# Query rows turned a stage early, the first queries sent back at once, ScalarE normalising, the row of maxima ahead of the last store

## The chip, the cores and the metric

One core of a Trainium2 chip runs the whole kernel. The metric is the device time of one execution in microseconds. The kernel before takes 3972.45 us, the median of three runs (3970.11 to 3986.83).

## The reference

A decoder layer on x of shape (4, 1024, 512): a self-attention against given keys and values, a cross-attention of 16 heads over a context of 1601 rows per batch, and a feed-forward part with 8 experts, each added to x. Only the front of the cross-attention matters here:

```python
x = x + self_attention(layernorm(x), k, v)
q = split_heads(layernorm(x) @ Wq.T + Wq_b)        # 4096 x 512
k = split_heads(ctx @ Wk.T + Wk_b)                 # 4 x 1601 x 512
v = split_heads(ctx @ Wv.T + Wv_b)
scores = where(mask == 0, -1e9, q @ k.T / sqrt(32))
x = x + (softmax(scores) @ v) @ Wo.T + Wo_b
```

where layernorm(x) = (x - mean) / sqrt(var + 1e-5) over each row, without learned factors.

## The kernel before

The kernel is a chain of blocks. At the end of a block all engines meet at a barrier; SP reaches it only when its DMAs have landed. Three blocks matter.

**The context stage** (`context_keys_values`, tiles named cxl_). For each of 4 batches and 4 groups q of 384 (the last 449) context rows, PE turns the rows of the next group (`turn`, L810), multiplies for the keys (`keys`, four products of 12 matmuls each) and for the values (`values`). Every fp32 number is held as a high and a low float32r part, so each product is three matmuls (`matmul3`, L44 to L46). ACT takes the high part out of PSUM, DVE the low part, and `finish_v` (DVE, L909) adds the bias of the values. SP stores keys and values. Two blocks of 512 rows of x1 for the next stage are loaded here (`q_rows`, the tensors probs) and normalised by DVE in the last batch. Before ACT and DVE begin they wait for both bias vectors (`bias_in`); DVE raises `cT_low` only behind that wait, and PE's first `turn` waits for `cT_low`.

**The query projection** (`project_queries`, tiles named pql_). 8 steps s of 512 rows, each with 4 products hd of 12 matmuls (one per chunk of 128 query columns). In step s PE also turns the rows of step s + 1, one 128-row piece (`turn`, L1160) ahead of each product. ACT takes the high part of the turned piece (`high`, L1208), DVE the low one (`low`, L1235), DVE adds the bias to a product (`query`, L1243), ACT makes the high half of that (L1219), POOL the low half (`split_q`, L1139), and SP stores a whole step's queries (L1118). DVE also takes the mean and variance of the rows of step s + 2 at hd 0 (`statistics`, L956 to L961), POOL the power -0.5 of it, and DVE normalises the four pieces at hd 2 (`normalize`, L967). The rows of step 0 are turned at the start of the block, ahead of the first product.

Inside this block the first maxima of the cross-attention are found too: 64 slots, each one matmul of scores (`mx`, L1013) and one DVE reduction (`read`, L1020). They need the keys of head group 0 (`load_keys`) and the first 512 queries of batch 0, which SP reloads from DRAM out of chunk 0 (`load_queries`, L999). Three slots go with each hd from step 2 on:

```python
FIRST_MX, SLOTS_AT = 2, 3
n = SLOTS_AT * (DC * (s - FIRST_MX) + hd)
```

At the end SP stores the last step's queries, then sends the row of maxima to DRAM (L1124) and back into the queries' tile (`put_row`, L1005), and waits for all of it.

**The cross-attention** (tiles named xa_) starts behind that barrier with the scores of unit 0 (L1476). SP's queue works in the order of its program: what stands behind a wait there is not sent before it. The name queries is one tensor that holds, by turns, the context's turned rows, the query weights and the queries of a head group.

## Time and profile before

| What | Value |
|---|---|
| Median of 3 runs (lowest, highest) | 3972.45 us (3970.11, 3986.83) |
| The profiled execution, its own time | 3982.51 us |
| Its span | 3980.7 us |
| Busy: PE | 3805.0 us (96%) |
| Busy: DVE, POOL, ACT | 2418.8, 1484.6, 1425.7 us |
| Mean granted clock of PE | 0.982 of full |

Times of a row are microseconds from the span's start. In a timeline a row is the start, the length, the engine and line, the operation, output <- inputs and their shapes; in brackets stands how long the engine was idle before it, and what ended that. A row with x4 is four instructions merged. SPq is SP's queue that issues DMAs. A row of a tile gives least/median/greatest length in ns. In a table of stretches each engine has its busy time and count, then come PE's granted clock as a share of full speed, the mean busy share of the 16 DMA engines and what they moved.

### The profile page before, as it was taken

To read this page: it belongs to the slowest core of one execution; us is meant where nothing else is said; L and a number is where in the kernel's file an instruction comes from. 1 tells how busy PE (TensorE), PEld (TensorE's weight loads), DVE (VectorE), ACT (ScalarE), POOL (GpSimd) and SP (SyncE) were. 2 spreads that over 40 slices of the span, in tenths; PEclk is the share of its full clock that TensorE was granted. 3 is DMA by queue.
4 is the path that set the end of the run, shared out by engine and by line. 5 is a ranking of instruction groups with operands and counts; after the bars stand their busy time and mean duration, and the time that the engine had idled before them with its cause. 6 is when DMAs were issued, how large, how long until landed. Compare 5 with 4: busy or idle time off the path is not lost. (4 is left out here: it accounts for less than half of the span.)

```text
span 3980.7 us, 63499 instructions
## 1 busy us (share of the span) xinstructions
PE 3805.0 (96%) x19001; PEld 2545.6 (64%) x19161; DVE 2418.8 (61%) x6240; ACT 1425.7 (36%) x1769; POOL 1484.6 (37%) x836
## 2 busy tenths in 40 slices
PE   8999999999987899999999999999999999988997
PEld 6888888888875444444444444444444777766875
DVE  6444444444447587888888888888887533424235
ACT  3112212133222344555545555545554312113332
POOL 1000000000012577666677666677664122220033
PEclk9999999999999999999999999999999999998999
DMA  4000000155554422221122222222202343237588
GB/s 153 32 32 32 32 32 32 61 169 178 196 159 146 110 53 56 56 50 34 40 47 55 56 56 56 56 53 55 56 20 81 124 147 111 102 107 265 163 291 282
DMA packets 224580, 381.59 MB, mean 96 GB/s; under 512 B 17448, under 2 KB 101960, under 8 KB 224332
## 3 DMA queue, kind: packets, MB, share of 16 engines
q1 hardware_dynamic: 197100, 309.73, 26.9%
q0 software_dynamic: 13120, 43.00, 3.0%
q10 hardware_dynamic: 14112, 25.70, 1.7%
q8 instruction: 137, 2.24, 0.2%
q14 instruction: 111, 0.91, 0.1%
HBM read 229.71 MB, written 148.66 MB: 95 GB/s over the span
## 5 line engine op out<-in xcount | busy, mean ns | idle before, releaser
L1020 DVE CUSTOM_DVE_ANT_0 xf_unread<-xa_mx_ps,mask_q 128x402 bf16<-128x402 f32 x1984 | 1034.4, 574 | 297.7 <-PE xa_mx_ps L1013 168.2
L1608 ACT ACTIVATE probs<-xa_scores 128x1024 f32<-128x1024 f32 (+1 forms) x416 | 417.2, 1023 | 417.4 <-PE xa_scores L1482 377.2
L1608 ACT ACTIVATE xa_probs<-xa_scores 128x1024 f32<-128x1024 f32 (+1 forms) x416 | 417.1, 1023 | 400.9 <-PE xa_scores L1482 353.2
L1443 POOL TENSOR_TENSOR xa_sums<-xa_sums,xa_probs 128x1024 f32<-128x1024 f32 x220 | 519.5, 2381 | 18.1 <-POOL xa_sums L1443 14.6
L1443 POOL TENSOR_TENSOR xa_sums<-xa_sums,probs 128x1024 f32<-128x1024 f32 x220 | 519.1, 2380 | 19.0 <-POOL xa_sums L1443 14.5
L1482 PE MATMUL xa_scores<-mask_t,ident_b 128*128 128x512 bf16 (+1 forms) x1505 | 500.8, 388 | 5.3 <-issue 0.2
L1013 PE MATMUL xa_mx_ps<-xa_kp,queries 96*128 96x402 f32 x1024 | 366.4, 419 | 0.8
L1013 PE MATMUL xa_mx_ps<-xf_kp,queries 96*128 96x402 f32 x960 | 343.2, 419 | 3.9 <-DVE xf_maxima L1020 3.6
L1476 PE MATMUL xa_scores<-queries,xf_kp 97*128 97x512 f32 (+1 forms) x832 | 285.0, 424 | 20.7 <-ACTq L1630 13.3
L1013 PEld LDWEIGHTS xa_mx_ps<-xa_kp,queries 96*128 96x128 f32 x1024 | 181.7, 189 | 171.3 <-DVE xf_maxima L1020 111.5
L1476 PE MATMUL xa_scores<-queries,xa_kp 97*128 97x512 f32 (+1 forms) x832 | 284.7, 423 | 1.8 <-ACT probs L1608 1.8
L1482 PEld LDWEIGHTS xa_scores<-mask_t,ident_b 128*128 128x128 bf16 (+1 forms) x1664 | 123.0, 100 | 244.9 <-issue 212.3
L1013 PEld LDWEIGHTS xa_mx_ps<-xf_kp,queries 96*128 96x128 f32 x960 | 171.0, 189 | 163.4 <-DVE xf_maxima L1020 106.1
L248 POOL TENSOR_TENSOR sa_rstd<-sa_var,sa_power 128x1 f32<-128x1 f32 x32 | 17.6, 550 | 674.1 <-DVE sa_var L433 674.1
L380 ACT ACTIVATE sa_pT_high<-sa_pT_ps 128x512 fp32r<-128x512 f32 x128 | 73.0, 596 | 532.8 <-PE sa_pT_ps L298 532.8
L44 PE MATMUL sa_scores<-weights,sa_nT_high 128*128 128x512 f32 x512 | 205.5, 401 | 7.5 <-DVE sa_nT_low L441 7.5
L44 PE MATMUL sa_o_ps<-sa_v_high,sa_pT_high 128*128 128x512 f32 x512 | 208.9, 408 | 1.1 <-DVE sa_pT_low L458 1.1
L1476 PEld LDWEIGHTS xa_scores<-queries,xf_kp 97*128 97x128 f32 (+1 forms) x832 | 149.5, 187 | 87.4 <-ACT xa_probs L1608 26.0
L46 PE MATMUL sa_scores<-weights,sa_nT_low 128*128 128x512 f32 x512 | 204.1, 399 | 0.0
L45 PE MATMUL sa_scores<-queries,sa_nT_high 128*128 128x512 f32 x512 | 203.6, 398 | 0.0
L46 PE MATMUL sa_o_ps<-sa_v_high,sa_pT_low 128*128 128x512 f32 x512 | 200.6, 392 | 0.0
L45 PE MATMUL sa_o_ps<-sa_v_low,sa_pT_high 128*128 128x512 f32 x512 | 199.3, 389 | 0.0
(382 smaller groups left out, 7377.1 us busy)
## 6 DMA issues: line engine op xcount, KB each, us to landing
ex_src<-sorted_in SPq DMA_DIRECT2D x78, 256.0 KB
sorted_out<-ex_made ACTq DMA_DIRECT2D x78, 256.0 KB
queries<-qT_high SPq DMA_DIRECT2D x30, 512.0 KB
xf_kp<-kT_high SPq DMA_DIRECT2D x16, 800.5 KB
xa_kp<-kT_high SPq DMA_DIRECT2D x16, 800.5 KB
rows<-in_ctx SPq DMA_DIRECT2D x16, 768.0 KB, 4.7
values<-cxl_v SPq DMA_DIRECT2D x48, 256.0 KB
kT_high<-cxl_kT_high SPq DMA_DIRECT2D x12, 768.0 KB
```

What stands on the lines that cost most here:

```text
L44: pe.matmul(out, lh, rh, start=start, stop=False)
L45: pe.matmul(out, lh, rl, start=False, stop=False)
L46: return pe.matmul(out, ll, rh, start=False, stop=stop)
L248: pool.tensor_tensor(rstd[:, :], var[:, :], power[:, :], ALU.pow).then_inc(root, 1)
L380: act.activation(pT[0][:, j * KB:(j + 1) * KB, :], pT_ps[j % 2][:, :, :], ACT.Copy).then_inc(pT_high, 1)
L1013: return pe.matmul(out[:, 0:MKEYS], qp[0:MAXROW, j, first:first + P], kp[0:MAXROW, j, MFIRST[kb]:MFIRST[kb] + MKEYS], start=True, stop=True)
L1020: return dve.tensor_tensor_reduce(out=unread[slot % 2][:, :], in0=scores[:, 0:MKEYS], in1=mask_q[:, half * QB + qt, MFIRST[kb]:MFIRST[kb] ...
L1443: pool.tensor_tensor(sums[pr][:, :, :], left[pr][:, :, :], right[pr][:, :, :], ALU.add).then_inc(pool_added, 1)
L1476: pe.matmul(scores[pr][0:keys, jj, :], kp[par][0:ROWS97, j, kt * P:kt * P + keys], qp[par][0:ROWS97, j, queries], start=True, stop=False)
L1482: last = pe.matmul(scores[pr][0:keys, jj, :], ident_b[0:keys, 0:keys], mask_t[0:keys, kt, queries], start=False, stop=True)
L1608: act.activation(prob[ring][pr][0:keys, :, :], scores[pr][0:keys, :, :], ACT.Exp, scale=SCALE).then_inc(exped, 1)
```

## The change

Five edits, all in the two stages above.

1. The bias wait is split in two (`k_bias_in`, `v_bias_in`). ACT waits for the keys' bias at its first key product, DVE for the values' bias at its first `finish_v`; neither waits at the start of the stage.
2. In the last context group, which has no group behind it to turn, PE turns the 4 pieces of the first query rows, ACT and DVE split them into `first_x`, a part of the tensor queries (`turn_queries`, `high_queries`, `low_queries`). DVE's statistics and normalising of the two blocks of query rows move by a group. The query projection starts with its first product. The values' stores go out one by one as each piece is done.
3. Chunk 0 of the queries of steps 0 and 1 is stored at once, the reload for the maxima waits for that store and for the 4 products of step 0 (they read `first_x`, where the reloaded queries go). The values of head group 0 are loaded in step 2. The 64 slots go over 23 products, from hd 2 of step 1 to hd 0 of step 7.
4. ACT normalises the rows (`normalize_row`), two pieces ahead of the last high half of a step and two behind it, with a scale and an offset per row; POOL makes the offset with a second instruction. DVE's statistics stand at hd 1 and have one small instruction more.
5. In the last step SP sends the row of maxima and its way back ahead of the last queries, and stores those in two parts.

```diff
-                act.wait_ge(bias_in, 32)
-                dve.wait_ge(bias_in, 32)
+                        act.wait_ge(k_bias_in, 16)
+                    dve.wait_ge(v_bias_in, 16)
...
-                    sp.wait_ge(v_done, before(b, q) + TILES[q] + 1 + TILES_B)
-                    for dst, src in parts:
+                    for r, (dst, src) in enumerate(parts):
+                        sp.wait_ge(v_done, before(b, q) + r + 2 + TILES_B)
                         sp.dma_start(dst, src).then_inc(v_stored, 16)
...
+                def turn_queries(r):
+                    pe.wait_ge(normed, 1)
+                    pe.wait_ge(cT_low, before(B, 0) + max(r - 1, 0) + 3)
+                    for dc in range(DC):
+                        last = pe.transpose(banks[:, r % 2, dc * P:(dc + 1) * P], q_rows[0][:, r, dc * P:(dc + 1) * P],
+                                            ident[:, :])
+                    last.then_inc(turned, 1)
...
+    def normalize_row(self, act, out, rows, s, r):
+        act.wait_ge(self.root, s + 3)
+        return act.activation(out[:, r, :], rows[:, r, :], ACT.Identity, bias=self.offset[:, r:r + 1],
+                              scale=self.rstd[:, r:r + 1])
...
-        n = SLOTS_AT * (DC * (s - FIRST_MX) + hd)
-        return range(min(max(n, 0), SLOTS), min(max(n + SLOTS_AT, 0), SLOTS))
+        n = DC * s + hd - MX_FROM
+        whole = MX_END - MX_FROM
+        return range(SLOTS * n // whole, SLOTS * (n + 1) // whole) if 0 <= n < whole else range(0)
...
+                def first_queries(half):
+                    sp.wait_ge(first_stored[half], 32)
+                    sp.wait_ge(made, DC)
+                    load_queries(sp, qT, 0, first.qp, slice(half * BANK, (half + 1) * BANK), queries_in[half])
...
-                for r in range(R):
-                    turn(0, r)
+                pe.sem_inc(turned, R)
...
+                    if s == steps - 1:
+                        first_row()
+                        store(s, slice(0, DC - 1), stored)
+                        store(s, slice(DC - 1, DC), stored)
+                    else:
+                        store(s, slice(1 if s < 2 else 0, DC), stored)
```

PE at the seam of context stage and query projection, before (L1160 are the transposes of the query rows, L44 to L46 a product):

```order
L747 UNCONDITIONAL_BRANCH
L1151 UNCONDITIONAL_BRANCH [waits barrier_Pool_Activation_PE_DVE_SP_release]
L1160 MATMUL pql_banks<-ident,probs 128x128 x8
L1160 MATMUL pql_banks<-ident,probs 128x128 [waits pql_low_n]
L1160 MATMUL pql_banks<-ident,probs 128x128 x3
L1160 MATMUL pql_banks<-ident,probs 128x128 [waits pql_low_n]
L1160 MATMUL pql_banks<-ident,probs 128x128 x3
L1160 MATMUL pql_banks<-ident,probs 128x128 [waits pql_low_n]
L1160 MATMUL pql_banks<-ident,probs 128x128 x3
L44 MATMUL pql_outs<-pql_nT_high,queries 128x512
L45 MATMUL pql_outs<-pql_nT_low,queries 128x512
L46 MATMUL pql_outs<-pql_nT_high,queries 128x512
```

and with the change, where L1261 are the same transposes:

```order
L748 UNCONDITIONAL_BRANCH
L1253 UNCONDITIONAL_BRANCH [waits barrier_Pool_Activation_PE_DVE_SP_release]
L1261 MATMUL pql_banks<-ident,probs 128x128 [waits pql_low_n]
L1261 MATMUL pql_banks<-ident,probs 128x128 x3
L44 MATMUL pql_outs<-queries 128x512
L45 MATMUL pql_outs<-queries 128x512
L46 MATMUL pql_outs<-queries 128x512
```

The sixteen transposes of the first rows are gone from between the barrier and the first product; the ones that stay belong to step 1.

ACT from the end of step 1 into step 2, before (L1208 high of turned rows, L1219 high of a product):

```order
L1208 ACTIVATE pql_nT_high<-pql_banks 128x4x128 [waits pql_turned,pql_made]
L1219 ACTIVATE pql_qT_high<-pql_q 128x512 [waits pql_q_done]
L1208 ACTIVATE pql_nT_high<-pql_banks 128x4x128 [waits pql_turned,pql_made]
L1219 ACTIVATE pql_qT_high<-pql_q 128x512 [waits pql_q_done]
L1208 ACTIVATE pql_nT_high<-pql_banks 128x4x128 [waits pql_turned,pql_made,pql_stored0]
L1219 ACTIVATE pql_qT_high<-pql_q 128x512 [waits pql_q_done]
L1208 ACTIVATE pql_nT_high<-pql_banks 128x4x128 [waits pql_turned,pql_made]
```

and with the change (L1308 and L1325 are these two, L1040 is the normalising of a piece):

```order
L1308 ACTIVATE pql_nT_high<-pql_banks 128x4x128 [waits pql_turned,pql_made]
L1040 ACTIVATE probs<-probs,pql_ln_offset,pql_ln_rstd 128x512 [waits pql_ln_root] x2
L1325 ACTIVATE pql_qT_high<-pql_q 128x512 [waits pql_q_done]
L1040 ACTIVATE probs<-probs,pql_ln_offset,pql_ln_rstd 128x512 [waits pql_ln_root] x2
L1308 ACTIVATE pql_nT_high<-pql_banks 128x4x128 [waits pql_made,pql_turned,pql_first_stored0,pql_stored0]
L1325 ACTIVATE pql_qT_high<-pql_q 128x512 [waits pql_q_done]
L1308 ACTIVATE pql_nT_high<-pql_banks 128x4x128 [waits pql_turned,pql_made]
```

Two pieces are normalised ahead of the last high half of the step and two between it and the first turned piece of the next step.

SP's queue in the opening of the query projection, before (xf_kp keys, xf_vg values, L1118 a step's stores, L999 the reload):

```order
L1106 DMA probs<-x 128x4x512 [waits pql_turned]
L989 DMA xf_kp<-kT_high 32x4x1601 x2
L989 DMA xf_kp<-kT_low 32x4x1601
L992 DMA xf_vg<-values 128x12x128
L993 DMA xf_vg<-values 65x128
L1106 DMA probs<-x 128x4x512 [waits pql_turned]
L1118 DMA qT_high<-pql_qT_high 128x4x512 [waits pql_low_q]
L1118 DMA qT_low<-pql_qT_low 128x4x512
L1106 DMA probs<-x 128x4x512 [waits pql_turned]
L1118 DMA qT_high<-pql_qT_high 128x4x512 [waits pql_low_q]
L1118 DMA qT_low<-pql_qT_low 128x4x512
L999 DMA queries<-qT_high 32x4x512 [waits pql_stored0]
```

and with the change (L1195 stores, L1075 the reload):

```order
L1188 DMA probs<-x 128x4x512 [waits pql_turned]
L1061 DMA xf_kp<-kT_high 32x4x1601 x2
L1061 DMA xf_kp<-kT_low 32x4x1601
L1195 DMA qT_high<-pql_qT_high 128x512 [waits pql_low_q]
L1195 DMA qT_low<-pql_qT_low 128x512
L1188 DMA probs<-x 128x4x512 [waits pql_turned]
L1075 DMA queries<-qT_high 32x4x512 [waits pql_made,pql_first_stored0]
L1075 DMA queries<-qT_low 32x4x512
L1075 DMA queries<-qT_high 32x4x512
L1195 DMA qT_high<-pql_qT_high 128x3x512 [waits pql_low_q]
L1195 DMA qT_low<-pql_qT_low 128x3x512
```

The reload stands ahead of the other three chunks of step 0 and no longer behind the stores of step 1, and the values are gone from here.

## Rows read from the trace of the kernel before

**Rows 1.** Stretches in us: busy PE, PEld, DVE, ACT, POOL, then PEclk, DMA share, GB/s

```profile
824.00:826.00 2.00, 0.00 (x0) 0.00 (x0) 0.00 (x0) 0.00 (x0) 0.31 (x3) 0.94 0.17 14
...
1334.00:1336.00 2.00, 2.00 (x6) 0.80 (x4) 0.00 (x0) 1.34 (x2) 1.92 (x1) 0.50 1.04 205
```

**Rows 2.** Timeline, start of the context stage, SP's queue and PE

```profile
824.11 0.37 SPq L750 DMA_DIRECT2D cxl_k_bias<-in_L_xattn_Wk_b  x1
...
828.71 1.09 PE L810 MATMUL cxl_banks<-ident,rows 128*128 128x128 f32 x4 [6.57 <-DVEq L912]
```

**Rows 3.** Timeline, end of the context stage, DVE, SP's queue and PE

```profile
1152.46 0.69 DVE L909 TENSOR_TENSOR cxl_v<-cxl_outs,cxl_v_bias 65x512 f32<-65x512 f32 x1 [2.08 <-PE cxl_outs L46]
...
1153.17 2.33 SPq L770 DMA_DIRECT2D values<-cxl_v  x4
...
1158.47 1.94 PE L1160 MATMUL pql_banks<-ident,probs 128*128 128x128 f32 x8 [5.76 <-PEq L747]
```

**Rows 4.** Waits of SP's queue, 1150 to 1160 us: in total, times, longest

```profile
SPq L788 <- DMA values<-cxl_v: 2.5, 1, 2.5
```

**Rows 5.** Timeline, PE in steps 0 to 2 of the query projection

```profile
1165.12 0.78 PE L44 MATMUL pql_outs<-pql_nT_high,queries 128*128 128x512 f32 x1
...
1168.89 0.60 PE L1160 MATMUL pql_banks<-ident,probs 128*128 128x128 f32 x4
1169.25 0.47 PE L44 MATMUL pql_outs<-pql_nT_high,queries 128*128 128x512 f32 x1
...
1183.68 0.71 PE L1160 MATMUL pql_banks<-ident,probs 128*128 128x128 f32 x4 [4.70 <-DVE pql_nT_low L1235]
...
1187.60 0.40 PE L46 MATMUL pql_outs<-pql_nT_high,queries 128*128 128x512 f32 x1
...
1214.74 0.67 PE L1013 MATMUL pql_mx_ps<-xf_kp,queries 96*128 96x402 f32 x1 [16.37 <-DMA queries<-qT_high]
```

**Rows 6.** Timeline, SP's queue and DVE in steps 0 to 2

```profile
1165.91 10.21 SPq L993 DMA_DIRECT2D xf_vg<-values  x1
1176.23 0.39 SPq L1106 DMA_DIRECT2D probs<-x  x1
...
1186.49 2.47 DVE L956 BATCH_NORM_STATS2 pql_ln_stats<-probs 128x6 f32<-128x512 f32 x4 [0.34 <-DMA probs<-x]
...
1206.47 1.27 SPq L999 DMA_DIRECT2D queries<-qT_high  x1
```

**Rows 7.** Timeline, DVE in step 3 and the start of step 4

```profile
1255.86 2.47 DVE L956 BATCH_NORM_STATS2 pql_ln_stats<-probs 128x6 f32<-128x512 f32 x4
...
1258.96 0.75 DVE L1243 SCALAR_TENSOR_TENSOR pql_q<-pql_outs,pql_q_bias,any_key 128x512 f32<-128x512 f32 x1
...
1262.14 0.75 DVE L1243 SCALAR_TENSOR_TENSOR pql_q<-pql_outs,pql_q_bias,any_key 128x512 f32<-128x512 f32 x1
...
1265.92 1.92 DVE L967 TENSOR_SCALAR probs<-probs,pql_ln_mean_var,pql_ln_rstd 128x512 f32<-128x512 f32 x4 [0.57 <-POOL pql_ln_rstd L951]
...
1277.20 0.75 DVE L1243 SCALAR_TENSOR_TENSOR pql_q<-pql_outs,pql_q_bias,any_key 128x512 f32<-128x512 f32 x1
```

**Rows 8.** Timeline, ACT: a copy, and what follows it at once

```profile
1262.92 0.63 ACT L1219 ACTIVATE pql_qT_high<-pql_q 128x512 fp32r<-128x512 f32 x1 [2.05 <-DVE pql_q L1243]
1263.46 0.58 ACT L1208 ACTIVATE pql_nT_high<-pql_banks 128x512 fp32r<-128x512 f32 x1
```

**Rows 9.** Tile cxl_k_bias: ACT's copies that read a bias per partition

```profile
L868 ACT ACTIVATE cxl_kT_high<-cxl_outs,cxl_k_bias x64: 580/582/639, 833.2 to 1140.8; 128x384 fp32r<-128x384 f32 x48, 128x449 fp32r<-128x449 f32 x16
```

**Rows 10.** Timeline, SP's queue and PE in steps 5 to 7 and the hand-over

```profile
1291.99 0.37 SPq L1118 DMA_DIRECT2D qT_high<-pql_qT_high  x1
...
1307.31 0.37 SPq L1118 DMA_DIRECT2D qT_high<-pql_qT_high  x1
...
1320.62 0.37 SPq L1118 DMA_DIRECT2D qT_high<-pql_qT_high  x1
...
1331.10 1.19 PE L1476 MATMUL xa_scores<-queries,xf_kp 97*128 97x512 f32 x2 [13.30 <-ACTq L1630]
```

160 lines of the change are left out of this document (111 added, 49 removed).

## The prediction

> **What bounds the kernel now.** I read the table of stretches first, then the timelines of PE, DVE, ACT and SP's queue from 818 to 1345 us, and asked at each stop of PE what ended it. PE is the bound of the kernel as a whole; the change touches only places where it stands still or is held back. There are five.
>
> (A) The context stage opens with PE idle for 6.57 us, ended by a semaphore of DVE [rows 2]. DVE raises it behind its wait for both biases, which SP only begins to send at 824.11.
> (B) The context stage ends 5.3 us after DVE's last addition: SP sends the four stores of the last group's values in one go, 2.33 us, and then waits 2.5 us for them to land [rows 3, 4].
> (C) From 1158.47 to 1165.12 PE turns the first query rows with ACT and DVE in the loop; no product runs [rows 3, 5].
> (D) Before slot 0 PE is idle for 16.37 us, ended by the reload of the queries; before that it is idle 4.70 us for DVE [rows 5]. The reload stands in SP's queue behind the stores of step 1, its last part being sent at 1206.47 [rows 6].
> (E) After the last product PE is idle for 13.30 us [rows 10].
>
> Between D and E the chain over DVE sets the pace. Step 3 to step 4 takes 18.24 us (1258.96 to 1277.20, the same instruction) [rows 7]. It is made of 4 x 3.18 (1258.96 to 1262.14: bias of a product, ACT's two copies, low half, reductions), 3.10 of statistics (1255.86 to 1258.96) and some 2.4 of normalising with its wait for POOL (1.92 and 0.57) [rows 7]. That is 12.7 + 3.1 + 2.4 = 18.2, the whole step: PE's own work is hidden under it.
>
> **The change, part by part.** Against the profiled execution, negative is a gain.
>
> 1. Biases. The engines meet at about 824.1 [rows 2]; then PE needs only semaphores that are raised at once and a POOL memset, so I place its first transpose at 824.7: -4.0 us. The granted clock was 0.94 over 824 to 826, so it fell to the half level only near the end of that stretch, after over 3 us of idleness [rows 1]; with PE back after 2.6 us it should not fall. A resumption at half clock lasts 3.9 us (1183.68 to 1187.60) [rows 5] and wastes half of that: -1.9. Bounds: 0 (something else also holds PE, such as the keys' bias, which ACT needs at its first copy 4 us later) and -6.5. I take -5.9.
>
> 2. The four turned pieces in the last context group. Each costs PE 0.36 (1168.89 to 1169.25) [rows 5]: +1.4. ACT and DVE have the same two copies per piece as in every other group and wait for PE there (2.08 of idleness before a 0.69 addition) [rows 3]. Moved statistics and normalising (3.1 and 1.9) lie under the same waits; without that cover they would cost 5, but they sit ahead of additions that only PE can release.
>
> 3. The values' stores. Only the last of four is left behind the last addition, about 0.8 instead of 2.33; the 2.5 of landing stay [rows 3, 4]: -1.6.
>
> 4. The first rows. 1158.47 to 1165.12 goes: -6.65 [rows 3, 5]. But PE comes back after some 4 us of idleness, probably at half clock, and now the products pay it: 1.9 instead of about 1.0 before: +0.9. First product at about 1158.4.
>
> 5. Steps 0 and 1. The stop of 4.70 and its slow 3.9 us behind it (half lost) go: -6.6 [rows 5]. In their place the first piece for step 2 must come from ACT: statistics wait for hd 1 and for the rows (sent 4 us earlier now), then POOL twice. I reckon ACT's first piece ends about 1.2 us after PE wants it: +1.2. In sum -5.4.
>
> 6. The reload. PE comes to slot 0, now 1.5 steps on, at about 1180.4. Queue: rows of step 2 and 2.4 MB of keys from 1158.9. Keys move at 205 GB/s [rows 1], so they are in at about 1174; the two stores of chunk 0 (0.5 MB) at 1175.8; the reload is sent in 3.6 us (each part 1.27 [rows 6]) and lands 2 to 3 us behind: 1182.5. PE waits 2.2 instead of 16.37: -14.2, and no half clock behind it: -1.7. Bounds: no wait at all (-16.4) or one of 8 us, if the 1 MB of rows that SP sends just ahead holds it up as the load of 1176.23 was, which had not landed until 1186.49 [rows 6].
>
> 7. Normalising on ACT. DVE loses about 2.4 a step, and gains one small instruction, 0.1. But the two pieces behind the last copy stand in front of the next step's first high half, which DVE's low half waits for: they are on the same chain. The trace has no ACT instruction with scale and bias both per partition. Lower end: a plain copy of that shape, 0.63 long, next one 0.54 later [rows 8]: 1.1 for two. Upper end: with one bias per partition 384 columns take 0.58 and 449 take 0.639 [rows 9], which carried on to 512 gives 0.70, and 0.77 with a second such operand, 0.68 back to back: 1.4 for two. I take 1.4, since the form is nearer. Step: 12.7 + 3.2 + 1.4 = 17.3 instead of 18.24; four steps: -3.8. With 1.1 it would be -5.0. The Trainium skill ("ScalarE: Activation LUTs", What ACT_TABLE_LOAD costs) prices each per-partition operand at 93 ns on top of 186 ns and 0.833 ns a column, so 0.80 us a piece: by it moving this work to ACT is dearer than the plain copy suggests, and the sum is the one of the upper end. No run here shows that form yet. The pieces ahead of the copy cost nothing: ACT idles 2.05 there [rows 8], more than 1.4.
>
> 8. The slots. Spread over 23 products, 5 of the 64 fall in step 1; in steps 2 to 5 they hide under the chain as before, in step 6 (15.32) and step 7 (13.31) [rows 10] PE is the bound and saves 0.2 each, in step 1 they cost 1.3: +0.9.
>
> 9. The end. The row of maxima is out of the way, under step 7. What is late next is the last store: the low half of the last product is ready 2.8 us after PE's last product, which ended at 1317.80 (1331.10 less 13.30), for the store went out at 1320.62 [rows 10]; 0.5 MB behind 1.5 MB lands about 4.5 later, and PE starts 0.9 after the barrier: 8.1 instead of 13.30: -5.2. Bounds: -8 (the last store lands in 2.5, as in [rows 4]) and 0.
>
> Sum: -5.9 + 1.4 - 1.6 - 6.65 + 0.9 - 5.4 - 14.2 - 1.7 - 3.8 + 0.9 - 5.2 = -41.3. The profiled execution took 3982.5, so 3941 on its terms; it lies 10 above the median of the runs, 3972.45, and against that I forecast **3931 us**. Nothing behind the barrier changes, and the cross-attention is PE's.
>
> **Rivals.**
> - *The reload is late.* For: all sends share SP's queue, and the load of 1176.23 took 10 us behind the keys [rows 6]. PE waits 8 us and falls to half clock behind it: +5.8 + 1.9, so 3939. The Trainium skill ("DMA: Bandwidth & Descriptors", Queues, rings and completion order) has descriptors of one issuer consumed in ring order, which is this rival's mechanism.
> - *The chain over ACT grows.* If the first piece of a step comes late each time (POOL's second instruction, ACT's waits for two stores), steps 2 to 5 take 19.5: +8.8, so 3940. Against: POOL's answer came 3.78 us after the bias of hd 1 (1262.14 to 1265.92) [rows 7]; ACT asks for it 5.1 after.
> - *Larger.* PE's own 15.0 a step shows through instead: another -9, so 3922. For: step 6, without statistics, took 15.32 [rows 10].
> - *A part does not do what it says.* PE's opening wait of A is set by something other than the biases, or the tail by the stores alone: 3935 to 3937.
> - *Slower.* SP was held 10.21 us in one send with its queue full [rows 6]. The block now has six sends more. If each load of rows of steps 3 to 7 is held as long, PE stops each time and restarts at half clock: 5 x (10.2 + 1.9) = +60, so 3991. It decides from 6.4 us a step on (41 / 5 less 1.9). Against: other sends took 0.39, and the values whose small pieces filled the queue have moved away.
>
> **How the numbers follow.** Forecast 0.62, late reload 0.12, longer chain 0.09, larger 0.08, a part missing 0.07, slower 0.02. The bounds of parts 1, 6, 7 and 9 taken together reach from 3917 to 3948; this holds all but the last case and the tails. About 0.5% (20 us) is what a measurement of this kernel can tell from no change. Gain above that: 0.94; within: 0.05; slower by more: 0.01.
>
> **What would show it.** PE's first transpose of the context stage near 824.7 at full clock; first product 4 us after the last context matmul; idleness before slot 0 of 0 to 4 us; the bias of a product in steps 2 to 5 every 17.3 us; ACT's pieces 0.7 each; PE idle about 8 us ahead of the cross-attention. Wrong if PE's idleness before slot 0 stays above 10, or if steps 2 to 5 stay at 18.

## The result and the profile after

| | before | changed |
|---|---|---|
| Median of 6 runs (lowest, highest) | 3977.76 us (3970.11, 3986.83) | 3950.01 us (3944.36, 3953.85) |
| Ratio, 95% interval | | 0.9930 (0.9919 to 0.9941) |
| The profiled execution, its own time | 3982.51 us | 3949.41 us |
| Its span, mean granted clock | 3980.7 us, 0.982 | 3947.6 us, 0.986 |

The change is faster by 27.7 us in the medians and by 33.1 us between the profiled executions. The forecast was 3931 us, with 3917 to 3948 as its range: the time lies 19 us above the one and 2 us outside the other. About 8 of the 19 us are a real miss (41.3 forecast, 33.1 measured between profiled executions). The other 10 or 11 come from the reference point: the profiled execution of before stood 10 us above the median then known, that of the changed kernel stands at its median.

The stages before the change start up to 1.7 us earlier or later from execution to execution. In all tables and in the text, times of a stage are therefore shifted so that the last transpose of the self-attention stage falls on 820.19, as in the trace of before; the changed kernel's own rows stand 0.38 later. Rows in fences are as the profile has them.

| mark (us, shifted) | before | forecast | measured | off by |
|---|---|---|---|---|
| first transpose, context stage | 828.71 | 824.7 | 825.54 | +0.8 |
| last addition of the context stage ends | 1153.15 | 1148.65 | 1145.46 | -3.2 |
| first product, query projection | 1165.12 | 1152.4 | 1148.71 | -3.7 |
| slot 0 | 1214.74 | 1176.5 | 1174.05 | -2.4 |
| last product ends | 1317.80 | 1281.7 | 1290.42 | +8.7 |
| attention starts | 1331.10 | 1289.8 | 1298.63 | +8.8 |

The column "forecast" adds up the terms of the prediction to each mark. From the end of the context stage to slot 0 the changed kernel is ahead of the forecast, and 11 us were lost between slot 0 and the last product.

First the changed kernel's totals, from its page:

```profile
span 3947.6 us, 63765 instructions
...
PE 3813.9 (97%) x19160; PEld 2546.1 (64%) x19161; DVE 2409.6 (61%) x6222; ACT 1442.7 (37%) x1793; POOL 1486.7 (38%) x842
```

PE's stops in the changed kernel, from its timeline (start, length, row, idle time before and what ended it):

```profile
825.92 1.11 PE L811 MATMUL cxl_banks<-ident,rows 128*128 128x128 f32 x4 [3.40 <-SPq L776]
...
1089.33 0.66 PE L811 MATMUL cxl_banks<-ident,rows 128*128 128x128 f32 x4 [0.40 <-DVE queries L908]
...
1148.71 0.63 PE L1261 MATMUL pql_banks<-ident,probs 128*128 128x128 f32 x4 [3.30 <-DVEq L1360]
...
1164.92 0.64 PE L1261 MATMUL pql_banks<-ident,probs 128*128 128x128 f32 x4 [1.64 <-DVE pql_nT_low L1340]
...
1174.43 0.67 PE L1089 MATMUL pql_mx_ps<-xf_kp,queries 96*128 96x402 f32 x1 [2.83 <-DMA queries<-qT_high]
...
1189.31 0.45 PE L1089 MATMUL pql_mx_ps<-xf_kp,queries 96*128 96x402 f32 x1 [0.62 <-DVE xf_maxima L1096]
...
1197.17 0.45 PE L1089 MATMUL pql_mx_ps<-xf_kp,queries 96*128 96x402 f32 x1 [1.77 <-DVE xf_maxima L1096]
...
1299.01 1.19 PE L1580 MATMUL xa_scores<-queries,xf_kp 97*128 97x512 f32 x2 [8.21 <-ACTq L1734]
```

They answer to [rows 2, 3, 5, 10]: 6.57 became 3.40, 5.76 became 3.30, the stop of 4.70 became 1.64, the one of 16.37 became 2.83, and 13.30 became 8.21. The last two before the attention, 0.62 and 1.77 us, are a pair that comes back in each of the steps 2 to 5 (0.81 and 1.75 in step 4), each ended by VectorE's maximum (DVE xf_maxima). Such pairs were there before the change too, as 1.45 and 0.83 us in step 3; the longer stop is new in its length.

SP's queue, from the timeline; these answer to [rows 3, 6, 10]:

```profile
1145.87 0.34 SPq L771 DMA_DIRECT2D values<-cxl_v  x1
...
1168.15 0.34 SPq L1075 DMA_DIRECT2D queries<-qT_high  x1
1168.54 0.43 SPq L1075 DMA_DIRECT2D queries<-qT_low  x1
...
1282.73 0.33 SPq L1205 DMA_DIRECT2D row<-xf_max_row  x1
1287.17 0.72 SPq L1081 DMA_DIRECT2D queries<-row  x1
...
1294.01 1.19 SPq L1195 DMA_DIRECT2D qT_low<-pql_qT_low  x1
```

One store of values is left behind the last addition instead of four (2.33 us). The reload's sends take 0.34 to 0.43 us, not 1.27. The row of maxima is on its way back 6.8 us before the last send of queries.

Now a step of the changed kernel, which answers to [rows 7]. DVE's timeline, from one query sum (pql_q) at hd 0 to that of the next step:

```profile
1208.69 0.75 DVE L1350 SCALAR_TENSOR_TENSOR pql_q<-pql_outs,pql_q_bias,any_key 128x512 f32<-128x512 f32 x1
...
1211.97 2.47 DVE L1027 BATCH_NORM_STATS2 pql_ln_stats<-probs 128x6 f32<-128x512 f32 x4
...
1215.40 0.75 DVE L1350 SCALAR_TENSOR_TENSOR pql_q<-pql_outs,pql_q_bias,any_key 128x512 f32<-128x512 f32 x1 [0.19 <-issue]
...
1222.66 0.58 DVE L1096 CUSTOM_DVE_ANT_0 xf_unread<-pql_mx_ps,mask_q 128x402 bf16<-128x402 f32 x1 [0.92 <-PE pql_mx_ps L1089]
...
1223.95 0.75 DVE L1350 SCALAR_TENSOR_TENSOR pql_q<-pql_outs,pql_q_bias,any_key 128x512 f32<-128x512 f32 x1 [0.71 <-PE pql_outs L46]
...
1227.29 0.69 DVE L1340 TENSOR_TENSOR pql_nT_low<-pql_banks,pql_nT_high 128x512 fp32r<-128x512 f32 x1 [2.10 <-ACT pql_nT_high L1308]
...
1228.39 0.74 DVE L1350 SCALAR_TENSOR_TENSOR pql_q<-pql_outs,pql_q_bias,any_key 128x512 f32<-128x512 f32 x1
```

and ACT in the same stretch, the last query copy of the step (L1325), the two pieces behind it (L1040) and the high half that DVE waits for:

```profile
1224.74 0.63 ACT L1325 ACTIVATE pql_qT_high<-pql_q 128x512 fp32r<-128x512 f32 x1 [2.32 <-DVE pql_q L1350]
1225.28 1.50 ACT L1040 ACTIVATE probs<-probs,pql_ln_offset,pql_ln_rstd 128x512 f32<-128x512 f32 x2
1226.69 0.57 ACT L1308 ACTIVATE pql_nT_high<-pql_banks 128x512 fp32r<-128x512 f32 x1
```

The lump of statistics takes 3.43 us (1211.97 to 1215.40). The two pieces hold up the high half by 1.41 us (1225.28 to 1226.69), so DVE idles 2.10 us. And twice DVE waits for PE (0.92 and 0.71). The clock is seen in the table of stretches (PE, PEld, DVE, ACT, POOL busy, then PEclk, DMA share, GB/s). Two pieces of this step, behind PE's stop at the statistics, then the steps 2 to 5 as a whole:

```profile
1216.00:1218.00 2.00, 1.31 (x6) 1.13 (x7) 1.80 (x7) 1.12 (x2) 1.11 (x1) 1.00 0.00 0
1218.00:1220.00 2.00, 2.00 (x10) 1.74 (x8) 1.68 (x7) 0.38 (x1) 1.35 (x3) 0.53 0.00 0
...
1189.17:1208.69 19.52, 17.13 (x75) 13.75 (x75) 14.29 (x41) 7.29 (x12) 6.34 (x6) 0.91 0.58 188
1208.69:1228.39 19.70, 17.14 (x75) 13.81 (x75) 14.29 (x41) 7.39 (x12) 6.34 (x6) 0.91 0.48 171
1228.39:1246.60 18.21, 15.64 (x75) 12.45 (x75) 14.27 (x41) 7.28 (x12) 6.36 (x6) 1.00 0.47 174
1246.60:1266.31 19.71, 17.81 (x81) 14.76 (x82) 14.78 (x43) 7.40 (x12) 6.33 (x6) 0.91 0.29 107
```

PE's stop at the statistics ends at 1216.7. The granted clock is 1.00 up to 1218 and 0.53 over the next two microseconds, about its lower level (1.2 of 2.4 GHz), and comes back within the step. The three steps with a mean clock of 0.91 take 19.5 to 19.7 us, the one with 1.00 takes 18.2. Before the change it was 1.00 from 1224 to 1278.

### The profile page after: what moved, and what is told of

Same layout as the page of the kernel before. It is cut to its first block and busy times, and to the rows that moved or that the text cites. A ratio compares the mean times of both kernels' runs of the same rounds, so it can differ in the third digit from the quotient of the medians.

```text
span 3947.6 us, 63765 instructions
## 1 busy us (share of the span) xinstructions
PE 3813.9 (97%) x19160; PEld 2546.1 (64%) x19161; DVE 2409.6 (61%) x6222; ACT 1442.7 (37%) x1793; POOL 1486.7 (38%) x842
## 5 line engine op out<-in xcount | busy, mean ns | idle before, releaser
L1586 PE MATMUL xa_scores<-mask_t,ident_b 128*128 128x512 bf16 (+1 forms) x1664 | 549.6, 388 | 0.0
L1547 POOL TENSOR_TENSOR xa_sums<-xa_sums,probs 128x1024 f32<-128x1024 f32 x220 | 519.7, 2383 | 18.1 <-POOL xa_sums L1547 14.5
L1547 POOL TENSOR_TENSOR xa_sums<-xa_sums,xa_probs 128x1024 f32<-128x1024 f32 x220 | 519.6, 2382 | 18.2 <-POOL xa_sums L1547 15.6
L44 PE MATMUL sa_scores<-weights,sa_nT_high 128*128 128x512 f32 x512 | 205.3, 401 | 7.8 <-DVE sa_nT_low L441 7.8
L44 PE MATMUL sa_o_ps<-sa_v_high,sa_pT_high 128*128 128x512 f32 x512 | 208.9, 408 | 1.3 <-DVE sa_pT_low L458 1.1
L46 PE MATMUL sa_scores<-weights,sa_nT_low 128*128 128x512 f32 x512 | 203.8, 398 | 0.0
L46 PE MATMUL sa_o_ps<-sa_v_high,sa_pT_low 128*128 128x512 f32 x512 | 200.6, 392 | 0.0
```

What stands on the lines that cost most here:

```text
L44: pe.matmul(out, lh, rh, start=start, stop=False)
L46: return pe.matmul(out, ll, rh, start=False, stop=stop)
L1547: pool.tensor_tensor(sums[pr][:, :, :], left[pr][:, :, :], right[pr][:, :, :], ALU.add).then_inc(pool_added, 1)
L1586: last = pe.matmul(scores[pr][0:keys, jj, :], ident_b[0:keys, 0:keys], mask_t[0:keys, kt, queries], start=False, stop=True)
```

## The experiments

**Theories.** A lump is work that stands on an engine in one piece, here VectorE's statistics. A: the steps are slower because the two pieces behind the copy and the longer lump each make PE stop, and with two stops a step the granted clock falls; rivals are the lump alone, the slots that now start earlier, and the move to ACT as such. B: the 3 us that the context stage gained beyond the forecast come from the moved statistics; rivals are the values' stores and the biases. C, D and E put prices on the bias split, the order of the row of maxima, and the reload.

The table gives, for every run, the interval from the first query sum of a step to that of the next; steps 2 to 5 are those that the forecast put at 17.3. Where the statistics stand at hd 0 (before, bias_only, stat0, dve_norm, late_dve), step 5 has none in its interval and is not comparable (in halved, halved_late and late_both it has half of them), and the first query sum of every step stands some 3 us later for it. Where a kernel was run more than once, the median is given with the ratio to the runs of before on the same chip; where not, the time of one execution.

| run | slot 0 | steps 0, 1; 2, 3, 4, 5 | last product ends | attention starts | time, ratio (interval) |
|---|---|---|---|---|---|
| before | 1214.7 | 16.7, 32.9; 18.3, 18.2, 18.2, 15.9 | 1317.8 | 1331.1 | |
| changed | 1174.1 | 14.9, 20.5; 19.5, 19.7, 18.2, 19.7 | 1290.4 | 1298.6 | 3950.0, 0.993 (0.9919 to 0.9941) |
| again | 1174.5 | 15.0, 20.6; 19.5, 19.7, 18.2, 19.7 | 1290.8 | 1299.0 | 3944.4, 0.992 (0.9899 to 0.9933) |
| spread | 1174.2 | 14.6, 18.7; 17.1, 17.2, 17.2, 17.4 | 1280.4 | 1288.6 | 3937.4, 0.991 (0.9891 to 0.9924) |
| stat0 | 1174.5 | 15.2, 16.5; 20.0, 20.2, 18.8, 16.8 | 1291.9 | 1300.1 | 3951.7, 0.994 (0.9927 to 0.9960) |
| dve_norm | 1180.1 | 16.5, 18.3; 18.3, 18.1, 18.1, 15.9 | 1290.5 | 1298.8 | 3935.8, 0.991 (0.9887 to 0.9925) |
| ctx_stat | 1183.2 | 14.9, 18.5; 17.9, 18.2, 19.7, 19.7 | 1296.7 | 1304.9 | 3954.3, 0.994 (0.9925 to 0.9960) |
| bias_only | 1213.7 | 16.8, 34.0; 18.3, 18.3, 18.2, 16.0 | 1317.1 | 1330.4 | 3981.5 |
| whole_store | 1180.6 | 18.8, 23.4; 17.9, 19.7, 18.2, 19.7 | 1294.2 | 1302.4 | 3945.4 |
| values_one | 1177.4 | 14.9, 18.5; 17.9, 18.2, 19.7, 19.7 | 1290.9 | 1299.1 | 3948.6 |
| row_last | 1175.0 | 19.4, 16.5; 17.9, 19.7, 18.2, 19.7 | 1287.9 | 1301.1 | 3947.5 |
| late_slots | 1182.3 | 19.1, 15.5; 18.2, 18.2, 19.7, 18.2 | 1285.9 | 1294.1 | 3944.3 |
| halved | 1174.7 | 15.5, 15.4; 16.3, 16.6, 16.6, 16.1 | 1279.2 | 1287.5 | 3937.8, 0.991 (0.9889 to 0.9925) |
| halved_late | 1174.7 | 20.0, 15.7; 16.3, 16.6, 16.6, 16.1 | 1279.6 | 1287.8 | 3933.1, 0.988 (0.9866 to 0.9899) |
| late_both | 1183.3 | 19.7, 15.6; 16.6, 16.6, 16.6, 16.2 | 1279.7 | 1287.9 | 3934.1, 0.991 (0.9888 to 0.9922) |
| late_spread | 1181.6 | 14.6, 15.3; 17.4, 17.3, 17.3, 17.3 | 1279.7 | 1287.9 | 3935.2, 0.991 (0.9890 to 0.9923) |
| late_dve | 1187.0 | 16.4, 18.6; 18.3, 18.3, 18.3, 15.9 | 1290.1 | 1298.3 | 3936.2 |

### What sets the pace: spread, stat0, dve_norm

**spread**: the late pieces go behind the high copies of hd 0 and hd 1 of the next step.

```diff
+                        if hd < R // 2 and 0 < s and s + 1 < steps:
+                            normalize(s + 1, R // 2 + hd)
                         act.wait_ge(q_done, DC * s + hd + 1)
                         act.activation(qT_sb[s % 2][0][:, hd, :], q[:, hd % 2, :], ACT.Copy).then_inc(high_q, 1)
-                        for r in range(R // 2, R) if hd == DC - 1 and s + 2 < steps else ():
-                            normalize(s + 2, r)
```

> Edit against the changed kernel: the third and fourth piece of rows are normalised by ScalarE one and two query groups later, behind the turned piece's high copy, where ScalarE waits for VectorE, instead of back to back behind the last query copy of the step. Theory A (the steps of the changed kernel are 18.2 to 20.5 us, mean of steps 1 to 5 19.5, because the two pieces behind the copy, 1.5 us, hold VectorE's low parts, which PE then waits for, and because these stops let the granted clock fall): the VectorE waits for the high copies in the first query group of a step go from 1.6 to 2.1 us to under 0.6, steps 2 to 5 come to 17.0 to 18.3 us each, the clock stays at 1.00 from the third step on, and the kernel gains 5 to 8 us on the changed one (3942 to 3945). Rival (the lump of statistics in the second query group, 3.4 us, alone sets the pace and the clock): steps stay at 19 to 20 us and the time stays within 2 us of 3950.

The steps came to 17.1 to 17.4 us and the attention starts 10.0 us earlier. ACT's timeline (its waits for the query sums) and the table of stretches:

```profile
1217.44 0.63 ACT L1327 ACTIVATE pql_qT_high<-pql_q 128x512 fp32r<-128x512 f32 x1 [1.39 <-DVE pql_q L1350]
1217.97 0.58 ACT L1308 ACTIVATE pql_nT_high<-pql_banks 128x512 fp32r<-128x512 f32 x1
1218.45 0.81 ACT L1040 ACTIVATE probs<-probs,pql_ln_offset,pql_ln_rstd 128x512 f32<-128x512 f32 x1
1221.04 0.64 ACT L1327 ACTIVATE pql_qT_high<-pql_q 128x512 fp32r<-128x512 f32 x1 [1.78 <-DVE pql_q L1350]
```

```profile
1216.00:1236.00 20.00, 18.22 (x91) 14.96 (x90) 15.76 (x44) 8.73 (x16) 7.03 (x7) 1.00 0.57 205
1236.00:1256.00 20.00, 18.24 (x91) 14.93 (x91) 16.93 (x48) 8.15 (x14) 6.93 (x7) 1.00 0.35 128
```

A piece of 0.81 us stands in front of an idle time of 1.78 us: it costs nothing there. The high half follows its copy at once again, and the clock stays at 1.00. VectorE's longest wait for a high copy falls from 2.10 to 0.69 us, a little above the 0.6 expected. Theory A holds on the steps and the clock. The time (3937.4) is better than the 3942 to 3945 expected; against the changed kernel run again on the same chip (3944.4, below) the gain is 7.0 us, within the 5 to 8.

**stat0**: `STATISTICS_AT = 0`, against 1 in the changed kernel.

> Edit against the changed kernel: the statistics run in the first query group of a step again, as before the change, not in the second. Rival of theory A (the lump's place sets the pace): PE's stop of 1.75 us for the maximum in the second query group goes and steps 2 to 5 fall below 18.5 us. Theory A: the lump of 3.4 us and the 1.5 us that the two late pieces take now fall into one query group, so PE stops there once for longer (over 2.5 us), steps 2 to 5 stay at 19 us or above, and the time is within 3 us of 3950 or above.

Steps 2 and 3 stayed at 20.0 and 20.2, step 4 took 18.8 (19 or more was expected), PE's stop is 2.3 us (over 2.5 was expected), and the attention starts 1.5 us later: the lump's place is not the cause.

**dve_norm**: VectorE takes the statistics at hd 0 and normalises at hd 2, as before.

```diff
-        norm = RowNorm(sb, sem, R)
+        norm = LayerNorm(sb, sem, R)
...
+                        if hd == 2 and s + 2 < steps:
+                            normalize(s + 2)
```

> Edit against the changed kernel: VectorE normalises the rows in the third query group and takes the statistics in the first, as before the change; everything else stays changed. If the move to ScalarE costs more than it saves (theory A as a whole), steps 2 to 5 come to 18.2 to 18.5 us, as before the change, against 19.3 in the mean, and the kernel is 3 to 5 us faster than the changed one (3945 to 3947). If the pace comes from the slots, which now start six groups earlier and stand in every group, the steps stay at 19 us or above, and the time at 3950 or above. As the prediction had it (17.3 with ScalarE, 18.24 with VectorE) the kernel would be about 3.8 us slower than the changed one.

The steps are back at 18.1 to 18.3 with the clock at 1.00, so the slots do not set the pace. But the attention starts where it does in the changed kernel (1298.8): what the steps gain is lost in front. The first query sum came at 1160.6 instead of 1153.4, and VectorE's row shows why:

```profile
1157.04 2.47 DVE L993 BATCH_NORM_STATS2 pql_ln_stats<-probs 128x6 f32<-128x512 f32 x4 [5.45 <-DMA probs<-x]
```

The statistics at hd 0 make it wait for rows that are still landing, and stand ahead of the sum themselves (3.1 us); 1.6 us of the 7.2 were there at the first product. In the changed form, then, moving the work to ScalarE bought nothing. That this run took 3935.8 all the same is a matter of the stages behind, told below.

### Where the context stage gained: ctx_stat, values_one, bias_only

**ctx_stat**: the statistics and the normalising of the last context batch at the places of before.

```diff
-                    if last and q == 1:
-                        query_statistics(0)
+                    if last and q in (1, 2):
+                        normalize_queries(q - 1)
+                    if last and q in (0, 1):
+                        query_statistics(q)
```

> Edit against the changed kernel: in the last context batch VectorE takes the statistics of the first query rows and normalises them at the places of before. Theory B (the 5 us that the context part gained beyond the forecast come from here: a batch of statistics no longer stands behind the mask preparation and in front of the queries that the transposes wait for): PE idles 3.8 us again at the start of the last batch, with its first transposes at 1.11 us instead of 0.56, and the last transposed piece of the context part comes 5 to 6 us later than in the changed kernel. Rival (the gain comes from the values stored piece by piece): PE's idle time there stays under 1 us and the end of the part moves by less than 1 us.

PE's stop came back, and the stage ends 8.8 us later, more than the 5 to 6 expected. First its timeline in this run, then before the change, with DVE's rows that lead up to it:

```profile
1091.40 1.11 PE L811 MATMUL cxl_banks<-ident,rows 128*128 128x128 f32 x4 [3.82 <-DVE queries L908]
...
1134.97 0.63 PE L819 MATMUL cxl_banks<-ident,probs 128*128 128x128 f32 x4 [1.55 <-DVE queries L915]
```

```profile
1091.17 0.64 DVE L652 TENSOR_SCALAR cxl_mk_tile<-cxl_mk_zero,cxl_mk_weight 128x1601 bf16<-128x1601 bf16 x1
1091.72 2.46 DVE L956 BATCH_NORM_STATS2 cxl_ln_stats<-probs 128x6 f32<-128x512 f32 x4
...
1095.14 0.69 DVE L889 TENSOR_TENSOR queries<-cxl_banks,queries 128x512 fp32r<-128x512 f32 x1
...
1095.88 1.11 PE L810 MATMUL cxl_banks<-ident,rows 128*128 128x128 f32 x4 [3.81 <-DVE queries L889]
```

In group 0 of the last batch the mask preparation and the statistics stood one behind the other on DVE, in front of the low half that PE's next transposes wait for. PE idled 3.8 us, and its transposes then took 1.11 us instead of 0.66, the lower clock. The change moves the statistics one group on, where no mask is prepared, and the stop falls to 0.40. Theory B holds. The 8.8 us are the stop (3.4), a smaller one that also returns (0.89, before the change 0.88 at 1117.31), one of 1.55 and some 3 us of the lower clock. The one of 1.55 stands in front of a turned query piece (L819), which the kernel before does not turn in this stage; so against before the move is worth some 7.3 us. That fits bias_only, whose stage ends 5.7 us behind the changed kernel's without the four turned pieces (1.4). Yet the attention starts only 6.2 us later: steps 1 to 3 took 2.0, 1.6 and 1.5 us less than in the changed kernel, and step 4 1.5 us more.

**values_one**: the values' stores in one go again.

> Edit against the changed kernel: the values of a context group are stored when all are made, in sends one behind the other, as before the change, not each piece when it is made. The prediction gave 1.6 us for it, all of it between the last addition of the context part and the start of the next block (2.9 us in the changed kernel): that gap comes to 4.3 to 5.3 us. Rival (the context's end gained from this, too): the last addition itself moves by over 1 us.

The last addition does not move (1145.61), and the next block starts 5.6 us behind it instead of 2.9: 2.8 us for this edit, above the 1.6 forecast and a little above the 4.3 to 5.3 expected for the gap. SP's row shows it, 2.33 us of sends:

```profile
1146.48 2.33 SPq L771 DMA_DIRECT2D values<-cxl_v  x4
```

At the attention only 0.5 us of it is left; the last section shows what the steps did meanwhile.

**bias_only**: the kernel before with `bias_in` split in `k_bias_in` and `v_bias_in`, as in the diff ahead of the prediction.

> Edit against the kernel before: the bias semaphore split alone. Forecast of the prediction: the first transpose at 824.7 instead of 828.71, and 1.9 us more from an unbroken clock, 5.9 in sum. Theory C, as the changed kernel shows it: the first transpose 3.2 us earlier, some 0.4 us from the clock, so that the last transposed piece of the context part comes 3.4 to 4.0 us earlier than before, with PE's idle time of 3.8 us in the last batch kept.

The first transpose comes at 825.55, 3.2 us earlier, but the last of the stage only 2.0 us, below both forecasts. The stop in the last batch is kept, and the attention starts 0.7 us earlier: the reload of the queries, which then set the time of slot 0, gained only 1.1 us.

### Reload, row of maxima, slots: whole_store, row_last, late_slots

**whole_store**: the first steps' queries are stored whole, the reload is sent behind that.

```diff
-                    if s < 2:
-                        store(s, slice(0, 1), first_stored)
...
-                        store(s, slice(1 if s < 2 else 0, DC), stored)
+                        store(s, slice(0, DC), stored)
+                    if s < 2:
+                        first_queries(s)
```

> Edit against the changed kernel: the first two steps' queries are stored whole, and the first unit's queries are loaded again behind that store, not behind a store of the first chunk alone. Theory E (the slots can start when the reload has landed, and PE waits for it in the seventh query group): slot 0 comes 7 to 13 us later than in the changed kernel (1181 to 1187 against 1174), PE idles that much in front of it, and the attention starts 5 to 12 us later, since nothing behind takes the wait back. Rival (the steps behind have room, so a late start is made up for): the attention starts less than 3 us later.

Slot 0 came 6.6 us later, a little under the range, and the attention 3.8 us later, between theory E's 5 to 12 and the rival's 3. Its stop from the timeline:

```profile
1180.69 0.67 PE L1089 MATMUL pql_mx_ps<-xf_kp,queries 96*128 96x402 f32 x1 [6.63 <-DMA queries<-qT_high]
```

The stop is 3.8 us longer than the 2.83 of the changed kernel. Step 2 starts 5.4 us later; steps 2 to 5 take 1.6 us less, with two falls of the clock instead of three, and so leave 3.8 at the attention. The rest of the 16.37 us [rows 5] went with the reload's place ahead of the stores of step 1 and with the values' load, which no longer stands in front; no run tells these two apart.

**row_last**: the row of maxima behind one whole last store.

> Edit against the changed kernel: in the last step all four chunks of the queries are stored in one pair of sends ahead of nothing, and the row of maxima is sent behind them, as before the change. Theory D (the row's way out and back ends the block): PE idles 11 to 13.3 us in front of the attention against 8.21, and the attention starts 3 to 5 us later than in the changed kernel. Rival (the last store's landing sets the end, whatever comes first): less than 1 us.

SP's last sends and PE's row at the attention:

```profile
1291.72 0.51 SPq L1195 DMA_DIRECT2D qT_low<-pql_qT_low  x1
1292.27 1.12 SPq L1205 DMA_DIRECT2D row<-xf_max_row  x1
1298.43 0.72 SPq L1081 DMA_DIRECT2D queries<-row  x1
...
1301.75 1.19 PE L1579 MATMUL xa_scores<-queries,xf_kp 97*128 97x512 f32 x2 [13.26 <-ACTq L1733]
```

The idle time is 13.26 us against 8.21: 5.05 for this edit, as theory D and the prediction had it. The attention starts only 2.5 us later, less than the 3 to 5 expected. Step 1 took 16.5 us and not 20.5, but step 0 took 19.4 and not 14.9, though the edit touches neither: VectorE stood 2.50 us before the rows of step 2. With the first query sum 1.4 us earlier, step 2 starts 0.9 us earlier in sum, and steps 2 to 5 take 1.6 us less, with two falls of the clock instead of three.

**late_slots**: the slots as before, three to a group from step 2 on.

```diff
-        n = DC * s + hd - MX_FROM
-        whole = MX_END - MX_FROM
-        return range(SLOTS * n // whole, SLOTS * (n + 1) // whole) if 0 <= n < whole else range(0)
+        n = SLOTS_AT * (DC * (s - FIRST_MX) + hd)
+        return range(min(max(n, 0), SLOTS), min(max(n + SLOTS_AT, 0), SLOTS))
```

> Edit against the changed kernel: the slots of the maximum start with step 2 and go three to a query group until step 7, as before the change, not from the seventh group on with two or three each. Step 1 then has no slots and no wait for the reload: it comes to 15 to 17 us against 20.5. Theory (the slots' work is the same, so what step 1 loses the end gains): the last step is longer by about 1 to 2 us and steps 2 to 5 have 12 slots each against 11.4, so 0.3 to 0.5 us more each; the attention starts 0 to 4 us earlier, since the stop for the reload of 2.8 us and its half clock fall away. If the early start was worth its price, it starts later than in the changed kernel by 1 us or more.

The attention starts 4.5 us earlier, a little beyond the expected range. The first query sum comes 1.4 us earlier and step 1 is 5.0 us shorter, but step 0 is 4.2 us longer, so step 2 starts 2.2 us earlier; steps 2 to 5 take 2.8 us less, with one fall of the clock instead of three, and step 6 takes 0.7 more. Whether the early start itself brings on the falls, or only shifts them as other edits do, this one execution does not show.

### The improved versions: halved, halved_late, late_both, late_spread, late_dve, again

**halved** is spread with the statistics cut in two (and SP's increments ahead of the bias sends).

```diff
+                        if hd == STATISTICS_AT - 1 and s + 2 < steps:
+                            dve.wait_ge(rows_in[s % 2], 16 * ((s + 2) // 2))
+                            norm.first_statistics(dve, rows[s % 2], s)
                         if hd == STATISTICS_AT and s + 2 < steps:
                             statistics(s + 2)
```

> Edit against the run called spread: the statistics of a step are cut in two (two rows in the first query group, two rows, the gathering and the two small operations in the second), and the increments that SP makes for PE and VectorE stand ahead of its two bias sends. Theory A, second half (each of VectorE's lumps makes PE stop as far as it is longer than the two slots of the maximum that PE may run ahead): PE's stop of 1.76 us in the second query group falls under 0.7 us, steps 2 to 5 come to 16.0 to 16.8 us against 17.2, and the attention starts 2 to 5 us earlier than in spread. Theory C (the first transpose of the context part waits for SP's increments behind the bias sends): the first transpose comes 0.8 to 2 us earlier than in the changed kernel. Rival (the step is bound by the work of PE and VectorE, not by the stops): the steps stay at 17.0 to 17.3 us and only the start gains. Time 3931 to 3935 by theory A and C, 3936 to 3937 by the rival.

The steps 2 to 4 came to 16.3 to 16.6 us. PE's stop is 1.0 to 1.1 us, not under 0.7:

```profile
1228.26 0.45 PE L1093 MATMUL pql_mx_ps<-xf_kp,queries 96*128 96x402 f32 x1 [1.11 <-DVE xf_maxima L1100]
```

The attention starts 1.2 us before that of spread, less than the 2 to 5 expected, because the first query sum came at 1157.96 (VectorE stood 6.33 us before rows that had not landed). The time, 3937.8 us, lies above what either theory gave. Theory C falls: the first transpose stayed at 825.52 although SP's increments came before its sends. That the row names SPq as what ended the wait is no proof, then, that these increments set it. What does set 825.5 stays open; it stands between 825.52 and 825.55 in the changed kernel and in all fifteen runs.

**halved_late**: no first half of the statistics in step 0.

> Edit against the run called spread: the statistics of a step are cut in two as in the run called halved, but not in step 0, where VectorE stood before rows that had not landed (the first query sum came 4.4 us later there); the increments of SP stand where the changed kernel has them. Theory: step 0 comes back to 14.6 us with its first query sum at 1153.6, steps 2 to 5 stay at 16.3 to 16.6 us, and the attention starts at 1283 to 1286 against 1288.6 in spread and 1287.5 in halved. If the two effects hide each other (the reload then holds slot 0 again), it starts at 1287 or later. Time: 3932 to 3936, with a scatter of 5 us from the attention and the experts, which no edit touches.

The first query sum came at 1153.45 as expected, but step 0 then took 20.0 us, and slot 0 and all behind it stood where they did in halved. The attention's start is that of the case named last, but its cause is another: slot 0 waited only 0.79 us for the reload, and VectorE stood before the rows of step 3, which the first half of the statistics needs at hd 0 of step 1:

```profile
1173.97 1.29 DVE L1040 BATCH_NORM_STATS2 pql_ln_stats<-probs 128x6 f32<-128x512 f32 x2 [4.12 <-DMA probs<-x]
```

**late_both, late_spread, late_dve**: halved_late, spread and dve_norm with the slots of late_slots.

> Edit against the run called halved_late: the slots start with step 2, three to a query group, as before the change. If the early start costs by itself (it stops PE for the reload and delays step 1), the 4.5 us of late_slots add to the gain of the spread pieces: the attention starts at 1282 to 1284.5 against 1287.8. If it cost only through the lack of room and the clock, step 2 starts 2 to 3 us earlier (1186 to 1187 against 1189.2), the steps 2 to 5 have 12 slots against 11.4 and come to 16.6 to 17.0 us, and the attention starts at 1285.5 to 1288.

> Edit against the run called spread: the slots start with step 2, three to a query group. Two causes: the attention starts at 1283 to 1285 against 1288.6. One cause: steps 2 to 5 at 17.1 to 17.6 us, the attention starts at 1286.5 to 1289.

> Edit against the run called dve_norm: the slots start with step 2, three to a query group, so that the steps 2 to 7 are those of the kernel before. Steps 2 to 5 come to 18.2 us each with the clock at 1.00, step 2 starts at 1186 to 1190, and the attention starts at 1294 to 1298 (1222.47 to 1331.10 took 108.6 us before the change, less the 5.0 of the end). Against late_slots (1294.1) that says what moving the normalising to ScalarE in the changed kernel's form is worth: 0 to 4 us, where the prediction had 3.8.

It is one cause. With the pieces spread the slots' start makes next to no difference: 1287.9 in both runs, against 1288.6 and 1287.8 with the early start. In late_both step 2 starts at 1189.0, not at the 1186 to 1187 expected, since VectorE stood 4.54 us before the rows of step 3. late_dve starts the attention at 1298.3, a little beyond its range, late_slots at 1294.1. In this setting the move to ScalarE is worth 4.1 us, but not by the pace: both have steps of 18.2 or 18.3, and late_slots one of 19.7. It lies in front of step 2, where VectorE stands 6.21 us before unlanded rows at hd 0 in late_dve, against 1.75 us at hd 1 in late_slots.

**again**: the changed kernel itself.

> The changed kernel itself once more, to see what of the differences between the runs belongs to the program and what to the execution: its attention took 1746.6 us in the profiled execution, against 1736.2 to 1744.1 in the other variants, though no edit touches it. If that is the program (its place in memory, its instruction stream), it takes 1745 to 1748 us again; if it is the execution, it falls anywhere between 1736 and 1747. The stages before it should repeat within 0.3 us.

Every mark up to the attention repeated within 0.5 us (0.3 was expected), and so did the pattern of the steps. The time was 5.6 us lower in the median (3944.4 against 3950.0). The attention, up to the first product of the stage behind it, took 1747.4 us after 1746.6: that part is the program's. In the other programs it lies between 1736.2 (dve_norm) and 1744.3. The experts' stage took 397.0 after 401.7 (396.7 to 407.6 over all runs): that part is the execution's. No edit touches either stage. Before the change the two took 1742.0 and 407.6 us, so of the 32.5 us that the changed kernel gained up to the attention 4.7 went in it and 5.9 came back with the experts. So a median here carries some 5 us of what the edits have nothing to do with, and the marks in front of the attention tell versions apart better than the times do.

The best version measured is halved_late, 3933.1 us, 0.988 of before. Its interval (0.9866 to 0.9899) does not overlap that of the changed kernel in the first set (0.9919 to 0.9941), and just touches the one of again. Between the five versions with spread pieces the attention's start differs by 1.2 us at most, and their times do not separate them, nor from dve_norm (3935.8). spread does it with the fewest lines.

## Why the prediction was right or wrong

**Part 7, normalising on ACT, is the step that failed.** It put a step at 12.7 + 3.2 + 1.4 = 17.3; steps 2 to 5 took 19.5, 19.7, 18.2, 19.7, that is 7.9 us more in sum. A step without a clock fall (18.2) is 0.9 above the forecast: the lump is 3.5 instead of 3.2 (query sum to query sum 6.68 at hd 1 against 3.18), and DVE waits 0.7 us for PE. The prediction took PE to be hidden under DVE's chain ("the whole step: PE's own work is hidden under it"). But PE may run only two slots ahead (two buffers for the maxima), so a lump on DVE stops PE, and what PE then lacks DVE waits for a group later. The other 4.3 us (1.3, 1.5 and 1.5) are the falls of the clock in three of the four steps, which the prediction had nowhere. Its own sign of being wrong, steps 2 to 5 that stay at 18, came true. That the stops bring on the falls is shown only in so far as the falls go with them: none came in spread, where the pieces no longer stand in the chain. The size of ACT's pieces was right: 1.41 us for two (1225.28 to 1226.69), taken as 1.4. The Trainium skill ("ScalarE: Activation LUTs", What ACT_TABLE_LOAD costs), whose price per operand gives 0.80, agrees with the 0.80 and 0.81 of a single piece. What was missed is the remedy in the same row: ACT idles 2 us in front of most copies, and spread put the pieces there.

**The rival "the chain over ACT grows"** had the right size (19.5 a step, +8.8, 3940) at 0.09. Its cause, POOL's second instruction or the waits for stores, was not the one: ACT's pieces start at once behind the copy (1225.28 behind 1224.74).

**Part 2 failed the other way.** "Moved statistics and normalising lie under the same waits" gave them 0; by ctx_stat they were worth some 7.3 us at the end of the stage. The trace of before held the stop of 3.81 us at 1095.88, but no timeline row that the prediction rests on lies between 830 and 1152. The four turned pieces were sized at 1.4, and nothing contradicts that.

**Part 1** was too large: 5.9 forecast, 3.2 for the first transpose, and 2.0 at the end of the stage in bias_only. The full clock that it counted on did not come: the four transposes at 825.92 take 1.11 us. **Part 3** was too small: 1.6 against 2.8 in values_one. The last send takes 0.34 us (1145.87), not 0.8, and the block ends 2.5 us behind it, where it had been 3.0 (1155.50 to 1158.47). **Part 4** was right: no transpose stands ahead of the first product but those of one piece, and the product comes 3.7 us before its forecast by the gains in front.

**Parts 5 and 6**: the wait before slot 0 is 2.83 us, forecast 2.2, which is in part luck: the three sends of the reload took 1.3 us instead of 3.6, but it landed 5.0 us behind them and not 2 to 3, and PE came 3 us earlier than forecast. PE did come back at the lower clock, which part 6 had excluded (mean of 0.83 over step 1, from 1168.70 to 1189.17); steps 6 and 7, up to the last product, took 24.5 us against 24.7 before, so the 3 of the 11 us that steps 2 to 5 do not explain lie in step 1. Slot 0 stands 2.4 us before its forecast. **Part 8** put the early slots at +0.9; late_slots gives 4.5 with the late pieces, 2.8 of it in steps 2 to 5 and so with the falls of the clock, and late_both about 0 without the late pieces. A price for one edit that holds only together with another was not in the sum. **Part 9** was right: 8.21 against 8.1 forecast, and row_last gives 5.05 against 5.2. The rivals of a late reload and of a slower kernel did not come: PE waited 2.83 us and not 8, and no load of rows held SP for more than 0.5 us (the send of 10.21 us was one of the values; that its queue was full is the prediction's reading, which no run tests).

So all terms up to the first product were off by 3.7 us in sum on the good side, those from there to slot 0 by 1.2 on the bad side, the end by 0.1, and the steps between by 11: the forecast missed by 8.8 at the attention because the first error took back part of the last. The bounds named (parts 1, 6, 7 and 9) add up to 3924 to 3948; the lower end of 3917 does not follow from them. The range was drawn about a profiled execution 10 us above its median, and nothing in it stood for a granted clock that falls inside the steps.

## What to carry to other kernels

Work moved off the engine that sets the pace should go where the other engine idles, not where it fits in the program: the same two instructions, moved from behind the last copy of a step to one and two groups later, started the attention 10 us earlier, falls of the clock included. Where two engines are coupled by two buffers, a lump on one is a stop of the other, so compare lumps and stops, not sums of busy time. Before pricing a move at nothing, read what stands behind the old place over its whole length: here the largest unforeseen gain lay there.
